# A fused adaLN transformer block on one core: landing transfers, norm placement, GELU's buffer, constant products at the start, and the maxima's rows

## The reference

```python
attn_in = _adaln(x, cond, ln1_w, ln1_b, g1_w, g1_b, b1_w, b1_b)     # x: (4, 512, 256)
x = _attn(attn_in, attn_in, sa_wq, sa_wkv, sa_wo, sa_bo) + x
cross_in = _adaln(x, cond, ln1_w, ...)
x = _attn(cross_in, _ln(context), ca_wq, ca_wkv, ca_wo, ca_bo) + x  # context: (4, 512, 192)
ffn_in = _adaln(x, cond, ln2_w, ...)
h = gelu(ffn_in @ ff_w1 + ff_b1, approximate=False)
x = h @ ff_w2 + ff_b2 + x
```

## Time and profile before

| | |
|---|---|
| median of 3 runs | 1145.44 us |
| the profiled execution | 1144.7 us, of which the span is 1142.9 us |
| PE busy | 1099.4 us (96%) |
| PEld, DVE, ACT, POOL busy | 786.5, 855.3, 638.0, 774.0 us |
| mean granted TensorE clock | 0.988 of full speed |

### The profile page before, as it was taken

One profiled execution on the slowest core, in us unless ns is written; L12 is line 12 of the kernel. 1 busy time (PEld: TensorE's weight loads), 2 busy tenths in 40 slices (PEclk: granted clock), 3 DMA queues, 4 the chain that ended last, 5 costly groups with the idle time before them and its releaser, 6 DMA issues.

```text
span 1142.9 us, 18646 instructions
## 1 busy us (share of the span) xinstructions
PE 1099.4 (96%) x6888; PEld 786.5 (69%) x6888; DVE 855.3 (75%) x1025; ACT 638.0 (56%) x895; POOL 774.0 (68%) x497
## 2 busy tenths in 40 slices
PE   7689999999999999999999999999999999989998
PEld 6456667776667777666766667776666667756887
DVE  5677787878787777778787777777787778676543
ACT  5455556665666555566565555555555555674521
POOL 3477788788678777688789766776777767654110
PEclk9799999999999999999999999999999999989999
DMA  6212111221221111211121112211121111300001
GB/s 183 61 30 75 38 41 45 70 48 34 51 73 40 38 38 31 59 38 38 26 64 38 38 38 50 58 33 32 31 70 38 38 38 38 93 1 1 20 19 37
DMA packets 65689, 52.36 MB, mean 46 GB/s; under 512 B 29120, under 2 KB 48576, under 8 KB 65344
## 3 DMA queue, kind: packets, MB, share of 16 engines
q1 hardware_dynamic: 63712, 49.59, 17.5%
q10 hardware_dynamic: 1888, 1.59, 0.5%
HBM read 15.22 MB, written 2.10 MB: 15 GB/s over the span
## 4 chain that ended last, share of the span: by engine, by line
PE 81%; DVE 7%; issue 4%; ACT 3%; POOL 2%; DMA 2%; SPq 2%; ACTq 0%; POOLq 0%; DVEq 0%
PE ps L862 16%; PE ps L711 11%; PE ps L712 10%; PE ps L713 10%; PE ps L809 6%; PE ps L840 5%; PE ps L850 5%; PE ps L815 5%; PE ps L811 5%; PE ps L813 4%; PE ps L945 3%; DVE neg_max L1036 2%; SPq L342 2%; DMA lo<-eo 1%; PE ps L727 1%
## 5 line engine op out<-in xcount | busy, mean ns | idle before, releaser
L537 ACT ACTIVATE probs<-ps 128x1024 f32<-128x1024 f32 x256 | 262.4, 1026 | 209.3 <-PE ps L815 185.5
L1036 DVE TENSOR_REDUCE neg_max<-ps 128x2 f32<-128x1024 f32 x256 | 301.7, 1225 | 80.9 <-PE ps L840 80.8
L412 POOL TENSOR_TENSOR acc<-acc,probs 128x1024 f32<-128x1024 f32 x128 | 304.6, 2380 | 17.7 <-POOL acc L407 0.4
L862 PE MATMUL ps<-probs,v 128*64 128x512 f32 x1024 | 230.7, 592 | 0.0
L407 POOL TENSOR_TENSOR acc<-probs 128x1024 f32<-128x1024 f32 x64 | 152.5, 2383 | 82.1 <-ACT probs L537 82.1
L417 POOL TENSOR_TENSOR eo<-tmp 128x512 f32<-128x512 f32 x62 | 89.2, 1439 | 137.9 <-DVE tmp L1063 129.0
L862 PEld LDWEIGHTS ps<-probs,v 128*64 128x64 f32 x1024 | 73.6, 137 | 145.8 <-issue 145.8
L1063 DVE TENSOR_TENSOR tmp<-ps,rope 128x1024 f32<-128x1024 f32 x128 | 150.6, 1212 | 3.5 <-PE ps L713 2.6
L809 PE MATMUL ps<-max_rows,pick 64*128 64x512 f32 x512 | 110.5, 422 | 11.1 <-DVE o_lo L1050 6.0
L840 PE MATMUL ps<-hi 64*128 64x512 f32 x512 | 106.8, 408 | 14.1 <-ACT hi L551 7.8
L711 PE MATMUL ps<-xn_hi,w_hi 128*128 128x512 f32 x256 | 108.2, 423 | 0.0
(11 more groups left out here) (113 smaller groups left out, 2269.1 us busy)
## 6 DMA issues: line engine op xcount, KB each, us to landing
lo<-eo SPq DMA_DIRECT2D x512, 64.0 KB, 2.0
w_raw<-pack_dram SPq DMA_DIRECT2D x16, 192.0 KB, 3.2
x<-x_dram SPq DMA_DIRECT2D x4, 512.0 KB, 10.8
w_raw<-pack_dram SPq DMA_DIRECT2D x8, 256.0 KB, 3.7
max_rows<-neg_max SPq DMA_DIRECT2D x128, 2.0 KB, 2.0
w_raw<-w_dram SPq DMA_DIRECT2D x2, 1024.0 KB, 5.6
out<-x SPq DMA_DIRECT2D x4, 512.0 KB, 2.9
ctx_in<-ctx_dram SPq DMA_DIRECT2D x4, 384.0 KB, 3.6
```

What stands on the lines that cost most here:

```text
L412: pool.tensor_tensor(acc[:, g % 2, :, :], acc[:, g % 2, :, :], probs[:, i, :, :], ALU.add).then_inc(added, 1)
L537: act.activation(probs[:, i, :, :], score_ps(i), ACT.Exp, scale=SCALE).then_inc(exped, 1)
L862: mm = pe.matmul(av_ps[DH * h:DH * h + DH, :], v[:, u % 2, kt, c:c + DH], probs[:, kt, h, :], start=(kt == 0), stop=(kt == TT - 1))
L1036: dve.tensor_reduce(neg_max[:, g % 2, :, i], peak_ps(i), AX.X, ALU.max, negate=True).then_inc(maxed, 1)
```

## The change

1. **Transfers.** A job is landed by two transfers of 256 KB, since a row of `lo` now takes the even and odd halves in turn. Job 1's sums go to a tile of their own, so they wait for no landing. `land_max` has four transfers: the maxima of heads 0, 1, 0, 1 go to rows 0, 32, 64, 96.
2. **Norms.** Rows are made one period after the statistics, right after `guess_inverse`; DVE takes the statistics after `normalise`; POOL refines after its last sum.
3. **GELU** writes back to its PSUM bank, `hid` is gone, and DVE reads PSUM. `hidden` waits for the split in place of the GELU. Two norms in this part move one block earlier, and POOL refines the last one in place of DVE.
4. **Start.** 10 and 6 constant products of 128x512; the four condition products are issued apart; jobs 0 and 1 are projected back to back; `cols` is loaded before `ada_w`, `ctx_ln` has its own semaphore, and `x[3]` and the first context are loaded later.
5. **Maxima's rows.** The rows' product uses two 32-row parts of one half of the array (rows 0 to 63 for steps 0 to 2, rows 64 to 127 for step 3). In step 2 a half of the maxima product follows it on the other rows, and its other half stands ahead of step 3's rows' product.

```diff
             def land(j):
                 u, k = j // 2, 1 - j % 2
-                sp.wait_ge(rotated, 2 * j + 1)
+                sp.wait_ge(rotated, 2 * j + 2)
...
-                            sp.dma_start(raw_qk[rows:rows + 32, g % 4, k, :], eo[at:at + 32, e, :])\
-                              .then_inc(landed, 16)
+                    sp.dma_start(raw_qk[:, g % 4, k, :], eo_of(j)[64 * a:64 * a + 64, :, :]).then_inc(landed, 16)
...
-                for h in range(2):
-                    sp.dma_start(max_rows[DH * h:DH * h + 1, :].bitcast(F32), neg_max[:, g % 2, h, :])\
+                for r in range(4):
+                    sp.dma_start(max_rows[32 * r:32 * r + 1, :].bitcast(F32), neg_max[:, g % 2, r % 2, :])\
...
-                act.activation(hid[:, f % 4, :], ps[:, (f + 3) % 4, :], ACT.Gelu,
+                act.activation(hid_ps(f), hid_ps(f), ACT.Gelu,
...
+            def lower(g, kt):
+                out = score_ps(kt)
+                for h in range(2):
+                    at = 32 * h + (64 if kt == 3 else 0)
+                    r = slice(at, at + 32)
+                    pe.matmul(out[:, h, :], pick[r, :], max_rows[r, :], start=True, stop=False)
...
-                for h in range(2):
-                    pe.matmul(out[:, h, :], pick[half[h], :], max_rows[half[h], :], start=True, stop=False)
-                for h in range(2):
+
+                heads = (1, 0) if kt == 3 else (0, 1)
+                for h in heads:
...
+                score_free(p, 2)
+                if is_pair(p + 1):
+                    peak_free(p + 1, 2)
+                lower(p, 2)
+                if is_pair(p + 1):
+                    peak(p + 1, 2, 1).then_inc(peaked, 1)
+                score(p, 2)
+                score_free(p, 3)
+                if is_pair(p + 1):
+                    peak(p + 1, 2, 0).then_inc(peaked, 1)
+                lower(p, 3)
+                score(p, 3)
+                if is_pair(p + 1):
+                    peak_free(p + 1, 3)
+                    peak(p + 1, 3, 0).then_inc(peaked, 1)
+                    peak(p + 1, 3, 1).then_inc(peaked, 1)
...
                 if is_pair(p - 1):
                     normalise(p - 1)
+                if p in stats_in:
+                    norm_stats(stats_in[p])
+                if is_pair(p - 1):
                     low_o(p - 1)
...
+            warm(10)
             modulate(0)
+            modulate(1)
             norm(0, 0)
             norm(0, 1)
             turn_rope()
-            modulate(1)
+            warm(6)
             project(0)
+            project(1)
```

More of the change, by code:

```diff
@@ L434, in period @@
                     add_probs(p, 2)
[L435 to L438, removed]
                     add_probs(p, 3)
-                if n is not None and not norm_at[n][3]:
-                    refine_rstd(pool, n)
+                if p in stats_in:
+                    refine_rstd(pool, stats_in[p])
                 if p in split_in:
@@ L602, in period @@
                     keep_av(p)
[L603 to L609, removed]
+                if p in stats_in:
+                    guess_rstd(stats_in[p])
+                if p in turned_in:
+                    norm(turned_in[p], 0)
+                    norm(turned_in[p], 1)
                 if p in v_in:
                     keep_v(v_in[p], 0)
-                if turned_late:
-                    norm(turned, 0)
-                if p in v_in:
                     keep_v(v_in[p], 1)
[L616 to L620, removed]
                 if p in (PAIRS - 3, PAIRS - 2):
@@ L670, in _ @@
             norm_rows(LAST - 1)
-            for f in range(3, 7):
-                gelu(0, f)
+            gelu(0, 3)
+            gelu(0, 4)
+            gelu(0, 5)
             norm(LAST - 1, 0)
+            gelu(0, 6)
             norm(LAST - 1, 1)
@@ L679, in _ @@
             norm_rows(LAST)
-            for f in range(1, 7):
+            for f in range(1, 6):
                 gelu(1, f)
             norm(LAST, 0)
+            gelu(1, 6)
             norm(LAST, 1)
@@ L879, in period @@
                     pe.wait_ge(maxed, 4 * (p + 1) + 4)
-                n = turned_in.get(p)
-                at_once = n is not None and norm_at[n][0] == p
-                if n is not None and not at_once:
-                    norm(n, 0)
-                    norm(n, 1)
+                if p in turned_in:
+                    norm(turned_in[p], 0)
+                    norm(turned_in[p], 1)
                 if is_job(p + 4):
@@ L896, in period, with warm @@
                     project_out(u - 1, 1)
+            def warm(count):
+                pe.wait_ge(const_ready, 6)
+                for _ in range(count):
+                    pe.matmul(ps[:, 1, :], pick[:, :], max_rows[:, :], start=True, stop=True)
+            warm(10)
             modulate(0)
+            modulate(1)
             norm(0, 0)
@@ L1108, in period @@
                     rotate(p + 4, 1)
-                if n is not None and is_pair(p + 2):
+                if is_pair(p + 2) and p in stats_in:
                     low_qk(p + 2)
@@ L1132, in _ @@
             turn(1)
+            norm_stats(2)
             rotate(2, 0)
```

207 lines of the change are left out of this document (106 added, 101 removed).

## The result

The changed kernel takes 1211.12 us (median of 4 runs, 1209.89 to 1211.95) against 1145.45: a ratio of 1.057 [1.055, 1.059], 66 us slower. I had forecast 1138, in a range of 1104 to 1172. Without part 5 the same change takes 1118.35 us (0.976 [0.974, 0.977]). So parts 1 to 4 win 27 us (28.7 against the 1147.0 of before beside that kernel), and the maxima's rows cost 93.

A forecast was written before the change was run, and what follows sets the result against it. PE's own dense list was taken to bound 605 to 995 us, with idle time elsewhere. Terms 19 - 13 - 4.5 + 1 - 2 - 5.7 = -5.2 us, called -7, gave 1138 us from 1145.45; range 1104 to 1172.

The forecast's parts named there:

- the maxima's rows: PE's pair phase, 63 periods: one slot saved, but a longer wait and weight load; +0.3 us a period, +19 us.
- The second rival: Pair phase: each change between 64-row and 32-row parts costs 0.107 us, seven more a period; +54 us, 1175 us; 22%.
- The saved slot: Pair phase: the wait for the reduction doesn't bind, so 0.233 us a period is won; -15 us, 1105 us; 20%.
- my case: Whole kernel: the main forecast, with +0.3 us a period in the pair phase; 1138 us, own range 1126 to 1147; 50%.
- slower first one: Pair phase before the change: 4.54 us counted as 19 slots of 0.233 us and a slower first slot.
- The wait for the reduction: Step 2 of a pair: PE waits for DVE's reduction of step 0 ahead of the rows' product, losing 0.43 us.
- my 0.1 for the weight load: Step 2's maxima product: its strided weight load is half exposed after the wait, +0.1 us a period.
- The start: Before the steady periods: waits for ACT's cast and for `keep_av` go, and clock is gained; -13 us, bounds -6 and -16.
- The third rival: Start: job 2's norm or the fourth x load keeps the first maxima product at 41 us; 1145 us, no change; 8%.
- Norms: Cross attention's x norms, 502 to 605 us: most PE idle time goes, -4.5 us; context norms may wait, +1 us.
- The end of attention: Period 61, PE's wait of 4.7 us for `low_o`: DVE's chain ends about 1.5 us earlier; -2 us, bounds 0 and -5.
- GELU and the feed-forward part: Feed-forward part: PE's waits for `hid_lo` go with GELU in its bank, -4.7 us, and -1 for the clock.

The follow-up runs named there:

- doublings: The kernel without part 5, with 32-row parts in the old order and four transfers, each 32-row product issued twice: 1264.58 us against 1206.14 with each once.
- halvings: The kernel without part 5, with 32-row parts in steps 2 and 3 only, 64-row halves in steps 0 and 1, four transfers: 1166.61 us, 1.018.
- the four-part kernel: The kernel without part 5, with the rows' products of steps 0 and 1 as four 32-row parts at the period's head: 1129.44 us, 0.986.
- the order-only kernel: The changed kernel with the rows' product back in 64-row halves and two maxima transfers, the new order kept: 1158.75 us, 1.011.

## Why the prediction was wrong

**The step that failed** is the choice of the case for the maxima's rows: that 32-row parts run beside a 64-row part and next to 64-row products at no cost, +0.3 us a period and +19 in all. Measured is +1.48 a period. The second rival (22%) had the right mechanism, and the removals, doublings and halvings above show it: 0.2 us for each change between 64-row and 32-row products, wherever it stands.

**The rival's price** was half of the true one, so that even the rival's 1175 us fell short by 36. I read the price off one distance, L840 to L850 in the earlier trace rows: 0.34 less 0.233. But a change lengthens two distances, that to the first product of the new shape and that from it to the next. The second half was in the same rows: at 599.70, behind a 128-row product, L809 lasts 0.50 us, and at 602.14, behind its own shape, 0.41. The "slower first one" among the 20 slots of my own count was just this. The lines around it, in the kernel before, give it as 0.34 us from 599.70 to the next product:

```profile
599.49 0.28 PE L713 MATMUL ps<-w_hi,o_lo 128*128 128x256 f32 x1
...
600.04 0.40 PE L811 MATMUL ps<-hi 64*128 64x512 f32 x2
```

With 7 x 0.2 = 1.4 a period and nothing of the wait left, the rival would have said 1145 - 24 + 63 x 1.4 = 1209 us.

**What spoke against it was no evidence.** The earlier trace rows show 96 rows behind 128 at the normal distance. That is a reading of another case: both are products over the whole array, with a distance of 0.24 us, while 64-row and 32-row products are parts of it, and the runs show their change to cost. The Trainium skill (TensorEngine Tiling (Array Packing), Tiling Modes, Key Properties) says that a change of tiling mode drains the engine. The runs agree that a change costs, with 0.2 us each; they do not show what the time goes to. The page gives no price, and I gave its rule less weight than a row that does not bear on it.

**The saved slot** (first rival, 20%, and my case) does not exist in after: L841's half started 0.43 behind L800, not beside it. Products of different shapes were not seen to start together. Four parts of one shape do run side by side, as the four-part kernel shows.

**The wait for the reduction** was right: 0.44 measured in the order-only kernel for 0.43 forecast. The total of that kernel's order, +0.65, is this with my 0.1 for the weight load (0.08 at L810, and 0.12 at the half of the maxima product, which came at 702.45) and the 0.12 at the sums, which I named and did not price. In after it is covered by the changes of shape.

**The start** was forecast at -13. In the kernel without part 5 it is -5.4 at period 0 and -4.3 in periods 0 and 1, together -9.7; the start varied by 1.2 us between kernels that have it in common. The wait for `hi` fell by 4.9, not by the whole 7.8 us: job 1's landing, issued at 29.58, was still what came last, not job 2's rotation, as I had said. Almost all of it hangs on the transfers: with eight of them the gain at period 2 is 2.9. I put their worth at the start alone ("nothing in the steady stretch"); with eight of them 6.6 us more go from period 2 to 36. These are no gain over before, though: its own periods 2 to 23 took 336.33 us with eight transfers. Why the changed kernel depends on them and before did not stays open: no run has eight transfers with the new order of the norms alone, or with the new start alone.

**A sum that does not come out.** The third rival's "+19 - 19 + 7" is +7, which is 1152 us; with the -6 that I gave as the bound for a late job 2 the parts are 19 - 6 - 11.2 = +1.8, about 1147 us. The 1145 of the text follows from neither. It decides nothing here: the start moved by 9.7.

**Norms:** forecast -4.5 and +1. Periods 24 to 35 gained 7.5 and 2 to 23 lost 0.2. **The end of attention:** -2 forecast, -3.3 measured, and its wait of 2.7 us stayed. **GELU and the feed-forward part:** -5.7 forecast, -6.6 measured, of which the place of GELU's result has 2.1. I had put all of it down to that place; the rest came with the norms and POOL's work. The cast from PSUM takes the forecast 0.69 us and in none of its 32 places more (compare); duration ns min/median/max, kernel after:

```profile
L1181 DVE CAST hid_hi<-ps x32: 678/691/693, 1112.9 to 1199.2; 128x512 fp32r<-128x512 f32 x32
L1183 DVE TENSOR_TENSOR hid_lo<-ps,hid_hi x32: 691/691/693, 1113.6 to 1200.0; 128x512 fp32r<-128x512 f32 x32
```

So parts 1 to 4 were forecast at -24 and gave -27: right in sum, too high for the start and too low for the norms.

## What to carry to other kernels

Count the changes of array shape in TensorE's list, not only its slots: between products on 64-row and on 32-row parts each costs 0.2 us here, almost a whole slot of 0.233, so a rearrangement that saves one slot and adds two changes loses. Read a price off both distances around an edge, the one to the first product and the one behind it, and from instruction means, since the busy share hides it. And when a large change mixes parts, run it without the suspected one: 1118.35 us is the fastest version here, and it was inside the change.

## What the runs showed of the hardware

- Four products on the four 32-row parts start together (711.56, x4), and the next product comes as soon as behind two (0.44 and 0.43 us). With each pair of 32-row products issued twice, an extra pair costs 0.223 us.
- A change between 64-row and 32-row products costs 0.2 us (0.197 with seven and with four changes in a period), about half in the distance to the first product of the new shape and half in the next distance.
- From a 128-row product to 32-row parts the distance is the same as to 64-row parts: 0.21 us after a 256-column product (711.35 to 711.56 above; 599.49 to 599.70 in before).
- A weight load is not brought forward over a change of shape; it starts with its product (601.41, 601.84).
- A wait in front of a product costs more than its length: the successor came 0.31 to 0.33 behind in place of 0.233, as its own weight load was no longer a slot ahead (at 702.18 and 714.19, behind the product that had waited).
- SP takes about 0.6 us for each issue of a landing transfer, whether of 64 KB (5.07 and 4.95 for 8) or of 256 KB (1.28 and 1.17 for 2).
